# A new written-out order of the lanes' pieces on all five engines

## The reference, cut to what matters

```python
x = x + tanh(g_xattn[0]) * L0_xattn(layernorm(x), ctx)   # 16 heads of 16
x = x + tanh(g_ffn[0])   * L0_ffn(layernorm(x))          # ternary weights, 8-bit activations, depthwise conv
x = x + tanh(g_xattn[1]) * L1_xattn(layernorm(x), ctx)   # 16 heads of 64
x = x + tanh(g_ffn[1])   * L1_ffn(layernorm(x))          # 8 experts, top 1
x = x + tanh(g_xattn[2]) * L2_xattn(layernorm(x), ctx)   # scores clamped
x = x + tanh(g_ffn[2])   * L2_ffn(layernorm(x))          # causal attention, then an MLP of 1024
x = x + tanh(g_xattn[3]) * L3_xattn(layernorm(x), ctx)
x = x + tanh(g_ffn[3])   * L3_ffn(layernorm(x))          # three residual blocks, dequantized weights
```

## Time and profile before

| | |
|---|---|
| median of three runs | 2888.14 us (2888.13 to 2888.65) |
| the profiled execution, its own time | 2895.3 us |
| its span | 2894.0 us |
| PE busy | 2628.6 us, 91% |
| DVE busy | 2205.1 us, 76% |
| ACT busy | 1673.5 us, 58% |
| POOL busy | 1141.8 us, 39% |
| mean granted TensorE clock | 0.966 of full speed |

### The profile page before, as it was taken

The page is one execution under the profiler, slowest core; times in us unless marked ns, Lnnn a source line. Parts: engine busy times, 40 slices in busy tenths (PEclk is TensorE's granted clock), DMA queues, the critical chain, the costliest instruction groups (busy, mean ns, idle before and its releaser), DMA issues.

```text
span 2894.0 us, 60821 instructions
## 1 busy us (share of the span) xinstructions
PE 2628.6 (91%) x23748; PEld 2135.5 (74%) x23748; DVE 2205.1 (76%) x4794; ACT 1673.5 (58%) x4529; POOL 1141.8 (39%) x1981
## 2 busy tenths in 40 slices
PE   6798988899798999899989999999999999997999
PEld 5676767777676777677768778787787878875787
DVE  7868687878777676877677776777778787766898
ACT  4565666666565656565465554565665565653444
POOL 2132323333443443323454444333343333323776
PEclk9899999999899999899999999999999999998999
DMA  5000000000011121100011211100000000001010
GB/s 185 3 23 9 20 12 16 16 12 18 18 49 48 54 65 34 36 18 20 10 49 51 63 56 51 39 22 15 19 18 22 16 24 10 26 3 35 30 34 27
DMA packets 84087, 92.14 MB, mean 32 GB/s; under 512 B 15252, under 2 KB 77208, under 8 KB 83800
## 3 DMA queue, kind: packets, MB, share of 16 engines
q1 hardware_dynamic: 75352, 59.91, 6.7%
q0 software_dynamic: 8448, 28.34, 3.4%
HBM read 65.36 MB, written 22.85 MB: 30 GB/s over the span
## 4 chain that ended last, share of the span: by engine, by line
PE 55%; DVE 31%; ACT 6%; POOL 4%; issue 4%; DMA 0%; another core or an unknown queue 0%; SPq 0%; DVEq 0%; POOLq 0%; ACTq 0%
PE psum L388 12%; PE psum L364 11%; PE psum L357 10%; PE psum L414 6%; DVE tiny L741 5%; DVE big L749 4%; PE psum L426 3%; PE psum L543 3%; PE psum L381 3%; PE psum L371 3%; PE psum L378 2%; DVE big L828 2%; DVE big L832 2%; DVE xn L722 2%; PE psum L537 2%
## 5 line engine op out<-in xcount | busy, mean ns | idle before, releaser
L388 PE MATMUL psum<-ident,big 128*128 128x128 f32 x2592 | 388.2, 285 | 77.2 <-ACT big L1228 35.1
L1228 ACT ACTIVATE big<-big 128x512 f32<-128x512 f32 x512 | 310.8, 631 | 188.8 <-DVE big L749 187.7
L388 PEld LDWEIGHTS psum<-ident,big 128*128 128x128 f32 x2592 | 297.2, 144 | 144.9 <-ACT big L1228 66.0
L741 DVE TENSOR_REDUCE tiny<-psum 128x8 f32<-128x1024 f32 x256 | 312.5, 1221 | 57.2 <-PE psum L414 51.9
L749 DVE TENSOR_TENSOR big<-psum,tiny 128x512 f32<-128x512 f32 x512 | 329.9, 686 | 8.8
L1394 POOL TENSOR_SCALAR tiny<-mv 128x1 f32<-128x1 f32 x224 | 54.7, 244 | 711.5 <-DVE mv L712 707.9
L414 PE MATMUL psum<-head_keys,small 64*128 64x256 f32 x2048 | 287.8, 404 | 29.4 <-ACT big L1235 18.2
L1411 POOL TENSOR_TENSOR head_keys<-big,head_rows 128x512 f32<-128x512 f32 x256 | 266.1, 1059 | 0.0
L1436 POOL TENSOR_TENSOR big<-big,tiny 128x512 f32<-128x512 f32 x128 | 138.4, 1085 | 319.0 <-DVE tiny L784 318.7
L414 PEld LDWEIGHTS psum<-head_keys,small 64*128 64x128 f32 x2048 | 186.2, 190 | 82.1 <-issue 59.2
L1272 ACT ACTIVATE big<-psum,tiny 128x128 f32<-128x128 f32 x512 | 181.8, 383 | 43.8 <-DVE tiny L779 41.1
(11 more groups left out here) (320 smaller groups left out, 6716.6 us busy)
## 6 DMA issues: line engine op xcount, KB each, us to landing
ctxT<-in_ctxT SPq DMA_DIRECT2D x64, 128.0 KB, 2.2
after_L_xattn<-x SPq DMA_DIRECT2D x64, 128.0 KB, 1.7
mixture_out<-spare SPq DMA_DIRECT2D x46, 128.0 KB
x_in<-in_x SPq DMA_DIRECT2D x32, 128.0 KB, 2.0
mixture_in<-xn SPq DMA_DIRECT2D x32, 128.0 KB, 1.7
x_in<-after_L_xattn SPq DMA_DIRECT2D x32, 128.0 KB, 2.1
bx_in<-after_L_xattn SPq DMA_DIRECT2D x32, 128.0 KB, 2.0
out<-bout SPq DMA_DIRECT2D x32, 128.0 KB, 1.7
```

Source lines behind the costliest of these rows:

```text
L388: last = pe.transpose(bank[:, k * P:(k + 1) * P], src[:, k * P:(k + 1) * P], identity)
L741: dve.tensor_reduce(top, s8, AX.X, ALU.max).then_inc(*t.dve.tell(p, f"{l}.top{r}"))
L1228: last = act.activation(flat, flat, ACT.Exp, scale=DH ** -0.5)
```

## The change

All ten strings of `ORDER` are replaced by others of the same length and with the same number of each digit, and nothing else in the file changes: no instruction, wait, tile or buffer. Each lane's own pieces keep their order; what changes is how the lanes are interleaved on each engine. 2733 of PE's 2754 pieces of part A stand at another place than before (by 37 places on average), 1907 of DVE's 1927, 2804 of ACT's 2830, 998 of POOL's 1020, 241 of SP's 277; of part B 376, 339, 182, 218 and 50. The first lines of some of the strings (the new file writes them in another sequence, so that some blocks show as added only, others as removed only):

```diff
 ORDER = {
     "pe": (
-        "3231232134121333222111332321321213123211400220232333101110003131313132310320102031023021321002001332"
+        "3132324132121111223312131131313223423023101112020333300022221111210120102002301312123200100112132132"
...
     "dve": (
-        "3123012403421321432423132421341421312233211310331131313131321232132102323202312100100200230021000003"
...
     "pool": (
-        "3120333222111321000313132321012203031312233333210011212112223001203300000331122331102323333300112201"
+        "2031333111222100032111212033221130301211211133232230320223133020310100001012323110221311311122020332"
...
     "pe_b": (
-        "3531516670740415152317526173452370621426045106123461027324652076542416572313765463715410260340356542"
...
     "dve_b": (
+        "7327302104615765072450327510341274657236102457015621404363156747253265101405427210425657167015075647"
```

More of the change, by code:

```diff
@@ new lines @@
+    "dve_b": (
+        "7327302104615765072450327510341274657236102457015621404363156747253265101405427210425657167015075647"
+        "6542671231034120463163041356254132453676573451206130723426453651205261246176374354037507365736120106"
+        "2501354237456723462175102650371347064136510745065626032763716231261723753725024075247302307240431247"
+        "1507510437540362674253716501702451430634061041640314"
+    ),
+    "act": (
+        "3313122321211111223322131311133313223222300101210133000303122122232110100103010122112120020122001133"
+        "2032131131231322332132133211213310230310131121011231032210201332030322221133103322102102123333203003"
+        "0022113321032123300011301201100100001100220211303213112232202103013320011212301322131121233211113312"
+        "0033021223022110022310202130133222231032200333300331133002312230212201010010013310033001331100202021"
+        "0211021233133222010323013110322103012231213321123311001303210231022021023020223332113232102211003233"
+        "1320000330223232321120130100101013313300122003231002000211202113231312130000132013112230131232113221"
+        "1211331102010221232032303101302210221013222102300233320300331013302123312332320103100210011000103300"
+        "3011032203232011122121223132322131121230021230021313013103112313122212323010302320301220301131303221"
+        "3022311202330033200331130312032202321312000011013031313001003322200110020121012201332132002003102031"
+        "2211313231230021032121011311331102120122020130302311213102232211002223202303303200233311223130232100"
+        "0331033232003113100001133003001332203112012120112123300320210230111310213132231131220320102211011021"
+        "2212023003203211011322032231001232230202002303331321230120200102333310102133331030100310000110322332"
+        "0132311312120022021003302311122313132003302311021120201311100120212233102213003132121203203111100220"
+        "2211231131033200011332210230321323010100333322322000031102221201323131331212333231121123132330130223"
+        "0232003112323122103000222211110200033101132130101223331302102330330322122131133222211003112030211121"
+        "0010033313200100203232130312300221132203022322002030112130302300102133223301121013333110113102230213"
+        "0032113210303100212220022002201211330132030221230101112330332133133220021230112121202302111100330230"
+        "1112130301020033313201222333130022012321030221322002003233303021100120332213031023330113113001010131"
+        "1003221020332112003100022312210220221120110332310103112213212003102333012022113231330030011131000033"
+        "2202212111021332100033213322002333130011300122223000001122120231230313131012033200331121100221003233"
+        "3001300032223101213012233022110031221022211113321332123323132001002122233113300003111122232002001331"
+        "1021301230102223231303022212331133010300222232001010210321033211233110233203301100111000033313220030"
+        "1120230131032203322113101222202331102311313032213322300130330232122010300121222002003310121103311210"
+        "0133133210203313232030010221123210000222203210132132301320110210103333112110012003331300003022311021"
+        "3021322330223110110220221111213321332233003102302100100313133223202000110131222330211211032010310233"
+        "1323020201023311332212230003022220231103123201330110021103323311211010200333010300302231120132013022"
+        "3020201131122322211110021002120002013323100300122122303331222023323310011231030112133100100213230021"
+        "0020333130221122313332203221310211023011023113332000012123233131001003333032202302310220030333002023"
+        "303232202002330332000033033303"
+    ),
@@ L216 @@
+    "act_b": (
+        "7320165740257032145763142705612043516473265104257610575467213120460431651253467345261073243605216734"
+        "50573616201523457346271625013074361740506237661237520524737203241751075034642376510410436014"
     ),
     "pool": (
[L218 to L220 removed]
@@ L221 @@
[L221 to L225, removed]
@@ new lines @@
+        "2031333111222100032111212033221130301211211133232230320223133020310100001012323110221311311122020332"
+        "2222130033333201010300101002211332201331111122033022220232013333302010100030011222231310131113112200"
+        "2222223130033333302101000101030221120200000103030000000110012211311322222222030313011033333332001221"
+        "0333000010001221310220011131133120112110222220102322232113333030323313322000100000013013322101300221"
+        "1131111133022022222220102330301313233030000000113221012213311111103032200222122122311300303300333231"
@@ new lines @@
+        "2000022111111333300200000000000000020221223110111023333330221222211101130300003333222212210000300333"
+        "1332111111200002003221222231111130333333202222211011110000003323333222122010000033331332121111010002"
+        "0032322212112103033332220211000000113333220001022113111130033002222123212011303333322221010000113333"
+        "2200022011113113123302000222221111303303333222201010001133332200002211313111032031002212212310123033"
+        "3330120212200011333300002212211331110330120022122211130230000002222131333311000022333322110011113003"
@@ L260 @@
+        "23322222030300003333"
+    ),
+    "pool_b": (
+        "7320371206571645024531704276520134571642036751425316042526751075170465246173041261304536243165751420"
+        "3362746352051261736450473657132065031427652341570623714061305746520637612613725327047523207401324750"
+        "143756027451360431064014"
     ),
     "sp": (
-        "3210312333212112000033331211221020003333111210222000333131112022002033303111312021232000231033213301"
-        "1231102220201300231032331021121212200000313323112212000032133022113210004331130322311122234001200403"
@@ L272 @@
[L272 to L281 removed]
+        "3120121131223323000011121322233300001112132233230000111212322330300011120122323313020103012011321102"
@@ L282 @@
+        "3221230332300100312011311202223203303000111212232033003010121322133020043110122113322241003332040031"
+        "10122112332420033040011213224033040121132240330401112342203300411244023031203"
     ),
     "sp_b": (
-        "35167042116562453423070755224416160037375241630754203716"
[L285 to L288, removed]
+        "73201654527104257106463351256241643773005612370472560314"
```

152 lines of the change are left out of this document (55 added, 97 removed).

## The result

The changed kernel takes 2847.31 us (median of four, 2844.29 to 2849.56) against 2888.14 (2887.11 to 2888.65): a ratio of 0.9858, with an interval of 0.9841 to 0.9875. That is 41 us faster; 31 were forecast. The profiled execution has a span of 2843.1 us, 51 under that of before. It is the fastest of the four, 3.0 us under their median, and that of before lay 7.2 above its own, so the traces show some 10 us more than the medians do.

A forecast was written before the change was run, and what follows sets the result against it. PE, busy 91% of the span, was taken as the bound, through its work, idle time and low-clock time. Terms -23 - 8 + 0 + 3 - 3 + 0 = -31 us took 2888.1 to 2857 us; range 2815 to 2898.

The forecast's parts named there:

- Items 1 to 6: PE's handoff waits in part A: more pieces of other lanes between cut waiting, -35.2 us counted, -23 taken.
- item 2: Wide attention's transposes on PE behind POOL: fewer close handoffs (24 to 11), so less waiting, -13.3 us.
- item 3: LayerNorm to its transpose on PE: waits fall from 31 to 19.3, -8.9 us.
- item 1: Exponential to transpose in narrow attention: waits fall from 38 to 33.4, -3.0 us.
- Item 7: PE's clock in part A: low-clock loss falls with idle time, 12% of 66 us, -8; bounds 0 and -66.
- Item 8: First 107 us, mostly loads and convolution: one lane's LayerNorm earlier, two later; 0 us, bounds -8 to +8.
- Item 9: Second plan: 14 of POOL's 16 scatters in a row, other lanes queue behind; +3 us, bounds -5 and +18.
- Item 10: End of part A: fewer PE pieces left with only two lanes, less waiting; -3 us, bounds 0 and -6.
- Item 11: Part B's handoffs between ACT and PE: more waits on some, fewer on another; 0 us, bounds -5 and +8.
- Rival 1: Gaps move to attentions' ends and restarts, 22 us; 2910 us; chance 0.19, shared with the scatter queue at 18 us.
- Rival 3: Low-clock stretches nearly vanish and all counted handoff gains of part A are kept; 2787 us; chance 0.12.
- Rival 2: Idle time lumps, some 10 us per thin stretch; 2888 us; chance 0.13, shared with the order doing nothing net.

The follow-up runs named there:

- Wide_later: The kernel before with only PE's string of part A edited: 16 wide-attention transposes moved up to three places later; 2889.53 us, ratio 1.0012.
- five_later: The kernel before with only PE's string of part A edited: 136 pieces of five handoff kinds moved up to three places later; 2975.76 us, ratio 1.0313.
- New part A: The kernel before with the five strings of part A new and those of part B old; 2840.95 us, ratio 0.984.
- fill_gaps: The kernel before, old order, with 197 idle matmuls on PE ahead of ten waits; 2880.28 us, ratio 0.9972.
- cut pairs: Part A cut after each lane's first eight passes, part B old; ahead/behind: old/old 2943.44, new/old 2907.56, old/new 2956.85, new/new 2921.64 us.

## Why the prediction came out right

The direction, the range and roughly the size were right (-31 forecast, -41 measured); the working of the largest term was not. That the sum came near is in part luck. Of its terms 1 to 6 gave some -16, the clock about -3, the end of part A -5, part B +5: together -19. The other 22 us stand in no term.

- **Items 1 to 6, -35.2 us of counted handoffs, two thirds kept.** This step failed: it made time out of the number of pieces between two others on PE. Wide_later changes that number for the wide transposes alone and gains nothing. In the changed kernel item 2's row rose by 3.1 us where -13.3 stood, item 3's fell by 3.8 (-8.9 stood), item 1's by 6.4 (-3.0), item 4's by 4.4 (-6.2), item 5's by 3.3 (-5.3). The seven rows together fell by 15.9 where -23 was taken, and all idle time from 107 us to the end of part A by 31.8. The sentence at the end of the prediction, that pieces are not time, was the right warning. The counts tell how often PE waits in items 1, 4 and 5 of five_later, and not what the order is worth.
- **Spreading of the bit stages over DVE**, a side remark in the prediction, fits about half: 22.5 of 41 us are left when 12 of the 16 multiply-adds of the convolution's outer taps are left out on DVE. So nearly half of the gain hangs on DVE's work there (its load, or the length of that handoff); the two light kernels don't show which digits bring it, and no run gives the new string to one engine alone.
- **Item 7, the clock, -8.** Between the two profiled executions the loss by the mean clock went from 0.034 x 2894 = 98 us to 0.029 x 2843 = 82. But that execution of the kernel before had a low clock: the 45 beside the experiments have medians of 0.968 to 0.969 on three chips, and the four of the changed kernel have 0.969. New part A has 0.971 against 0.969 on its chip, some 7 us less loss, worth 2 to 3 us at the price that fill_gaps gave. So the sign holds in part A at most, and the term was too large, in the slow time saved and in its price. PE's busy time fell by 19.7 us in the profiled pair, more than the clock's part alone, which the prediction had as a sign of being right.
- **Item 8, the start, 0.** Idle time fell by 1.8 us and the clock rose from 0.82 to 0.86; a gain of a few us that was not seen.
- **Item 9, the scatters, +3.** In the old surroundings they cost 8 us, with one wait of 9.39; in the new ones no LayerNorm waits behind them. What a block costs hangs on who stands behind it.
- **Item 10, the end of part A, -3.** In the last 80 us PE idled 9.8 us (2554.1 to 2634.4, busy 70.50) before; after, 4.4 (2498 to 2578.7, busy 76.26). -5.4.
- **Item 11, part B, 0.** +5 to +6, inside its bounds. The counts had pointed to more waits, but not to the right ones: of the handoffs counted, `xT` to `z` (39 to 58 close) waits 0.5 us less, and `bhT` (49 to 54) 1.8 more.
- **Rival 1** (waits move to the attentions' ends) didn't happen: the rows of L426 and L537 are 12.1 us after, 13.2 before. **Rival 3** neither: the clock is 0.971. **Rival 2** happened in the small: the second half's clock fell to 0.99, and its sign shows once, at the second plan (PE busy 1.14 of 5 us, then 0.50).
- **Its signs.** PE's idle time from 107 us to the place that answers to 2600 is 168 us (near 175 was asked for), the clock of 700 to 1400 us is 0.96, and the waits at L414 at the end of part A are fewer (0.9 us, where 3.9 were). The rows behind POOL (27.6, not 11) and at L843 (7.4, not 5) are not where they should be.
- **Its own range.** The lower end, -60, doesn't add up from what it names: -35, a third of 66, and the good ends of 8 to 11 (-8, -5, -6, -5) make -81.

The account is: first half -36 (medians of the cut pairs), second half -7 (traces: 8 us less once it runs, 1.8 more at its start), part B +5 (medians): -38, against -41 measured. The two uncut profiled executions are 49.1 us apart already at the last lane's last router matmul; 10 of that is the executions' own distance from their medians, and the rest of the difference to 36 no run takes apart. Nor is it shown what makes the part of the gain that DVE's work in the bit stages doesn't explain.

## What to carry to other kernels

Where in-order engines hand work round in a circle, an order is one thing over all of them. Moving pieces in one engine's string by the engine's own waits can cost more than a whole new order brings (five_later), and a piece moved away from one partner comes nearer to the next: count that one too. Judge a block of slow instructions, a gap or a slow-clock stretch by what stands behind it, and test that by moving only it. And take a change of several parts apart before keeping it: here part B's new strings gave back a ninth of what part A's had won.

## What the runs showed of the hardware

Filling PE's long gaps with matmuls that do nothing kept the clock up (0.966 to 0.979 over the span in the profiled executions, 0.968 to 0.976 by the medians), and made the kernel 0.28% faster though it does 197 matmuls more. In the new order it wasn't tried.
